# Mixture-of-experts block after attention: when GpSimd sends the experts' result rows

## The chip, the cores and the metric

The kernel runs on one core of one Trainium2 chip. The metric is the device time of one launch in microseconds (us). The kernel before takes 563.42 us (median of 3 runs, 561.5 to 564.76). The engines are called by these names: TensorE (PE in the profile), VectorE (DVE), ScalarE (ACT), GpSimd (POOL), and SyncE (SP), which here only starts DMA transfers.

## What is computed

4096 tokens of width 256 pass through an attention block with a residual, and then through a feed-forward block of 32 small experts, of which each token uses 4, beside one shared expert:

```python
x = x + _L0_xattn_ref(_layernorm(x), mask, ctx_2048, ctx_2048, wq, wk, wv, wo)
x = x + _L0_ffn_ref(_layernorm(x), router_weight, w_gate, w_up, w_down, sw_gate, sw_up, sw_down, sgate_w)

# inside _L0_ffn_ref, E, F, FS = (32, 96, 512), TOP_K = 4
probs = jax.nn.softmax(x @ router_weight.T, axis=-1)
topv, topi = jax.lax.top_k(probs, TOP_K)
topv = topv / jnp.sum(topv, axis=-1, keepdims=True)
g = jnp.einsum('th,ehf->etf', x, w_gate)
u = jnp.einsum('th,ehf->etf', x, w_up)
act = jax.nn.silu(g) * u
out = jnp.einsum('te,etf,efh->th', combine, act, w_down)
shared = jax.nn.silu(x @ sw_gate) * (x @ sw_up) @ sw_down
out = out + jax.nn.sigmoid(x @ sgate_w) * shared
```

## The kernel before

The program has three parts in time. First the attention, the router and the scattering: GpSimd sends each token's normalized row to four places of a DRAM table `sent`, ordered by expert. Then the expert loop, which this change touches. At last the shared expert's remaining products and the weighing of the experts' results.

In the expert loop the rows of `sent` are taken in 136 tiles of 128 rows, two tiles to a pair, 68 pairs (0 to 67). Every odd pair from 3 to 65 is mixed: its first tile holds four quarters of 32 rows, each for an expert of its own, and its weights are copied together beforehand (`gu_copy`, `dn_copy`). One pair goes through these steps:

- SyncE loads its rows into one of six buffers `loaded` (L366, L368).
- TensorE transposes them (L920), ScalarE copies the result to `gt` (L597).
- TensorE multiplies by gate and up (L944, L948), ScalarE applies SiLU to the gate (L603), VectorE multiplies gate and up into `act_e` (L1366, semaphore `act_e_ready`).
- TensorE transposes that product (L958), VectorE copies it (L1372, `act_et_ready`), TensorE multiplies by down (L972, L975, `down_psum`).
- VectorE copies the result from PSUM into `down_e`, one of four buffers of SBUF inside `arena2` (L1381, `down_ready`). The profile calls it arena.
- GpSimd starts two indirect DMA transfers for a pair (L480), one a tile. Each writes 128 rows to the places in DRAM (`returned`) that `back` names. They count up `down_sent`.

All engines run their own list in a fixed order, and wait on counting semaphores. VectorE's list for iteration `pair` is: the product of `pair` (L1366), the `down_e` copy of `pair - 4` (L1381), the copy of the transposed product of `pair - 1` (L1372), with the small steps that make `back` in the even iterations (L1395 to L1410) between them; in the odd iterations from 5 on two copies of down weights for a mixed pair (L1438) follow.

Two waits tie GpSimd's transfers to the rest. Before the copy of pair q + 4 into the same buffer, VectorE waits until both transfers of pair q have landed:

```python
                if pair >= DOWNS:
                    dve.wait_ge(down_sent[u], 32 * (pair // DOWNS))
```

And after the loop SyncE waits for all of `down_sent` (L372) before it loads the first results back for the weighing (L375). GpSimd has no other work during the loop and after it.

Of the kernel before, what the change touches and what calls it, by code (L numbers as in the profile page):

```python
# [35 lines left out]
def build_xattn_moe(nc, x, ctx, ctx_t, wq_t, wk_t, wv_t, wo_t, router_t, w_gate_up, w_down,  # L36
# [34 lines left out]
    with ExitStack() as stack:  # L71
# [181 lines left out]
        def wait(eng, name, count):  # L253
            if count > 0:
                eng.wait_ge(S[name], count)
# [47 lines left out]
        def _(sp):  # L303
# [51 lines left out]
            for pair in range(pairs):  # L355
                u = pair % RING
                first, size = column_of(pair), QUARTER if mixed(pair) else P
                _, at = nc.values_load_multi_w_load_instructions(
                    tile_row[0:1, first:first + (5 if mixed(pair) else 2)], engines=[mybir.EngineType.SP],
                    min_val=0, max_val=EXPERTS * tokens - size,  # L360
                    skip_runtime_bounds_check_because="a tile's first row is a row of an expert's "
                                                      "region, at most its count less a tile on")
                wait(sp, "gt_psum", pair - RING + 1)
                wait(sp, "back_ready", (pair - RING) // 2 + 1)
                for q in range(P // size):
                    sp.dma_start(loaded[size * q:size * q + size, u, 0, :].bitcast(F32), sent[bass.ds(at[q], size), :]) \  # L366
                        .then_inc(tile_in[u], 16)
                sp.dma_start(loaded[:, u, 1, :].bitcast(F32), sent[bass.ds(at[P // size], P), :]).then_inc(tile_in[u], 16)  # L368
# [15 lines left out]
        def _(pool):  # L384
# [87 lines left out]
            for pair in range(pairs):  # L472
                u = pair % DOWNS
                wait(pool, "back_ready", pair // 2 + 1)
                wait(pool, "down_ready", pair + 1)
                for s in range(2):
                    t = 2 * pair + s
                    if s == 1:
                        wait(pool, "act_e_ready", min(pair + 6, pairs))
                    pool.indirect_dma_start(  # L480
                        out=returned,
                        out_offset=bass.IndirectOffsetOnAxis(ap=back[:, t:t + 1], axis=0),
                        in_=down_e[u][:, s, :], in_offset=None).then_inc(down_sent[u], 16)

        @block.scalar
        def _(act):
# [121 lines left out]
            def experts_to_copy(pair):  # L608

                first = column_of(pair)  # L610
                more = 7 if mixed(pair + 2) else 0
                _, values = nc.values_load_multi_w_load_instructions(
                    tile_expert[0:1, first:first + 4 + more], engines=[mybir.EngineType.Activation],
                    min_val=0, max_val=EXPERTS - 1,
                    skip_runtime_bounds_check_because="a tile's first row over the rows of a region "
                                                      "is the number of an expert")
                copied_e[pair], copied_e[pair + 2] = values[0:4], values[7:11]
# [58 lines left out]
        def _(pe):  # L676
# [248 lines left out]
            def experts_of(pair):  # L925
                first = column_of(pair) + (4 if mixed(pair) else 0)
                _, values = nc.values_load_multi_w_load_instructions(
                    tile_expert[0:1, first:first + (1 if mixed(pair) else 2)], engines=[mybir.EngineType.PE],
                    min_val=0, max_val=EXPERTS - 1,
                    skip_runtime_bounds_check_because="a tile's first row over the rows of a region "  # L930
                                                      "is the number of an expert")
                return values
# [610 lines left out]
```

## Time and profile before

| what | value |
|---|---|
| median of three runs, without profile | 563.42 us (561.5 to 564.76) |
| span of the profiled execution, first to last instruction | 649.9 us |
| mean granted TensorE clock | 0.937 of full speed |
| GpSimd's transfers of the loop (L480) | 136, first at 324.9 us, last at 566.8 us |
| expert loop, by VectorE's products (L1366) | 314.0 to 550.4 us |

The page gives the span of the profiled execution and no other time of it. The span is 86.5 us longer than the median of the runs without a profile. A profiled execution is read for what waits for what, and for how long single instructions take. Its times are microseconds from the first instruction. Matmul ends are modelled.

### The profile page before, as it was taken

To read this page: it belongs to the slowest core of one execution; us is meant where nothing else is said; L and a number is where in the kernel's file an instruction comes from. 1 tells how busy PE (TensorE), PEld (TensorE's weight loads), DVE (VectorE), ACT (ScalarE), POOL (GpSimd) and SP (SyncE) were. 2 spreads that over 40 slices of the span, in tenths; PEclk is the share of its full clock that TensorE was granted. 3 is DMA by queue.
4 is the path that set the end of the run, shared out by engine and by line. 5 is a ranking of instruction groups with operands and counts; after the bars stand their busy time and mean duration, and the time that the engine had idled before them with its cause. 6 is when DMAs were issued, how large, how long until landed. Compare 5 with 4: busy or idle time off the path is not lost.

```text
span 649.9 us, 13112 instructions
## 1 busy us (share of the span) xinstructions
PE 575.3 (89%) x3884; PEld 435.9 (67%) x3884; DVE 353.5 (54%) x1169; ACT 251.0 (39%) x631; POOL 294.9 (45%) x502
## 2 busy tenths in 40 slices
PE   7999895985987867599999999899999998979997
PEld 7999784874876545255777666676677785455565
DVE  4468663663644662451445455454455545269985
ACT  4755451540533322001556455456555644101110
POOL 3011858158166688773055544555555555600000
PEclk8999987797798998799999989899999997979999
DMA  6578454253247194223345544455545551288863
GB/s 180 178 250 255 164 157 151 91 168 140 72 146 248 69 216 171 93 79 101 101 144 152 153 134 142 138 162 151 153 145 158 158 149 70 93 349 293 302 220 130
DMA packets 65956, 104.36 MB, mean 161 GB/s; under 512 B 9856, under 2 KB 52864, under 8 KB 65792
## 3 DMA queue, kind: packets, MB, share of 16 engines
q1 hardware_dynamic: 48160, 63.62, 32.9%
q0 software_dynamic: 12672, 35.14, 14.9%
q10 hardware_dynamic: 5056, 4.75, 2.3%
q8 instruction: 34, 0.56, 0.4%
q14 instruction: 34, 0.28, 0.2%
HBM read 59.84 MB, written 43.65 MB: 159 GB/s over the span
## 4 chain that ended last, share of the span: by engine, by line
PE 63%; another core or an unknown queue 13%; DVE 7%; issue 6%; ACT 4%; POOL 2%; DMA 2%; ACTq 1%; DVEq 1%; POOLq 0%; SPq 0%
PE bank L694 11%; PE bank L701 11%; PE bank L948 9%; PE bank L975 7%; PE bank L736 5%; PE bank L944 4%; PE bank L845 3%; PE bank L972 3%; PE bank L920 2%; PE bank L860 2%; PE bank L874 2%; POOL sent L444 1%; PE bank L958 1%; ACT hnt L625 1%
## 5 line engine op out<-in xcount | busy, mean ns | idle before, releaser
L480 POOL DMA_INDIRECT returned<-arena,back x136 | 130.7, 961 | 138.3 <-DVE arena L1366 63.4
L444 POOL DMA_INDIRECT sent<-rows,slot x128 | 125.2, 978 | 40.9 <-issue 28.2
L701 PE MATMUL bank<-hnt,ws_gu 128*128 128x512 f32 x256 | 117.7, 608 | 1.4 <-DVE arena L1381 1.4
L701 PEld LDWEIGHTS bank<-hnt,ws_gu 128*128 128x128 f32 x256 | 49.0, 195 | 55.6 <-issue 52.4
L948 PE MATMUL bank<-w_gu,arena 128*128 x416 | 85.8, 344 | 0.5 <-ACT arena L597 0.5
L948 PEld LDWEIGHTS bank<-w_gu,arena 128*128 128x128 f32 x416 | 66.8, 192 | 1.7 <-issue 0.8
L597 ACT COPY arena<-bank 128x512 f32<-128x512 f32 x68 | 39.4, 581 | 64.8 <-PE bank L920 35.1
L427 POOL TENSOR_TENSOR rstd<-var_eps,neg_half 128x4 f32<-128x4 f32 (+1 forms) x21 | 19.0, 907 | 91.6 <-DVE var_eps L1058 83.1
L1366 DVE TENSOR_TENSOR arena<-bank,arena 128x192 f32<-128x192 f32 x68 | 24.2, 355 | 65.8 <-ACT arena L603 51.7
L1381 DVE COPY arena<-bank 128x512 f32<-128x512 f32 x68 | 46.6, 685 | 22.8 <-remote 15.8
L505 ACT ACTIVATE act_t<-bank 128x512 f32<-128x512 f32 x24 | 14.3, 597 | 115.3 <-PE bank L701 86.5
L1484 DVE SCALAR_TENSOR_TENSOR resid<-arena,combine,resid 128x256 f32<-128x256 f32 x128 | 51.5, 476 | 9.1 <-DMA arena<-returned 9.1
L625 ACT COPY hnt<-w_gu 128x384 f32 x128 | 56.0, 514 | 0.0
L694 PE MATMUL bank<-w_hi_all,att_split 128*128 128x256 f32 x256 | 51.5, 304 | 3.0 <-issue 2.5
L694 PE MATMUL bank<-att_split,w_hi_all 128*128 128x256 f32 x256 | 46.1, 292 | 7.0 <-issue 5.7
L736 PE MATMUL bank<-ws_d,act_t 128*128 128x256 f32 x192 | 46.9, 405 | 4.7 <-DVE act_t L1075 3.5
L736 PEld LDWEIGHTS bank<-ws_d,act_t 128*128 128x128 f32 x192 | 39.1, 205 | 13.6 <-DVE act_t L1075 3.9
L920 PE MATMUL bank<-ident_r,loaded 128*128 128x128 f32 x272 | 45.3, 290 | 0.0
L603 ACT ACTIVATE arena<-bank 128x192 f32<-128x192 f32 x68 | 22.3, 328 | 53.4 <-PE bank L944 21.4
L694 PEld LDWEIGHTS bank<-att_split,w_hi_all 128*128 128x128 f32 x256 | 38.3, 200 | 5.9 <-issue 4.2
L694 PEld LDWEIGHTS bank<-w_hi_all,att_split 128*128 128x128 f32 x256 | 39.4, 201 | 3.6 <-issue 2.9
L920 PEld LDWEIGHTS bank<-ident_r,loaded 128*128 128x128 f32 x272 | 30.9, 142 | 10.4 <-issue 4.7
(188 smaller groups left out, 965.2 us busy)
## 6 DMA issues: line engine op xcount, KB each, us to landing
arena<-returned SPq DMA_DIRECT2D x16, 1024.0 KB, 6.7
loaded<-sent SPq DMA_DIRECT2D x104, 132.0 KB
w_gu<-w_gate_up SPq DMA_DIRECT2D x16, 384.0 KB
sent<-rows SPq DMA_DIRECT2D x4, 1056.0 KB, 6.4
loaded<-sent SPq DMA_DIRECT2D x128, 33.0 KB
resid<-x SPq DMA_DIRECT2D x16, 256.0 KB
att_plain<-ctx_t SPq DMA_DIRECT2D x16, 256.0 KB
att_plain<-ctx SPq DMA_DIRECT2D x16, 256.0 KB
```

The source lines that it names most:

```text
L444: pool.indirect_dma_start(out=sent, out_offset=bass.IndirectOffsetOnAxis(ap=slot[:, 2 * b + j, k:k + 1], axis=0), in_=rows[:, u, j, :], in ...
L480: pool.indirect_dma_start(out=returned, out_offset=bass.IndirectOffsetOnAxis(ap=back[:, t:t + 1], axis=0), in_=down_e[u][:, s, :], in_offs ...
L597: act.copy(gt[pair % 2].rearrange("p s c q -> p (s c q)"), gt_banks[pair % 2][:, :]) \
L625: last = act.copy(gu_copy[:, q, :, :], w_gu[:, :, bass.ds(copied_e[pair][q], 1), :] .rearrange("p c e f -> p c (e f)"))
L694: last = pe.matmul(out_view, stationary(s_part, c), moving(m_part, c), start=(n == 0 and c == 0), stop=(n == 2 and c == DC - 1))
L701: last = pe.matmul(bank[:, :], ws_gu[:, c, at:at + P], hnt[:, c, 512 * g:512 * g + 512], start=(c == 0), stop=(c == DC - 1))
L736: last = pe.matmul(sum_banks[t // 2][:, 256 * (t % 2):256 * (t % 2) + 256], act_t[:, f, P * t:P * t + P], ws_d[:, f, :], start=(f == 0 and ...
L920: last = pe.transpose(gt_banks[pair % 2][:, at:at + P].bitcast(F32R), loaded[:, u, s, P * c:P * c + P], ident_r[:, :])
L948: last = pe.matmul(view[:, s, :], rows_t[:, s, c, :], w_gu[:, c, bass.ds(e[s - 2 + len(e)], 1), :] .rearrange("p e f -> p (e f)"), start=( ...
L975: last = pe.matmul(bank[:, D * s:D * s + D], act[:, s, :], w_dn[:, bass.ds(e[s - 2 + len(e)], 1), :].rearrange("p e d -> p (e d)"), start= ...
L1381: dve.tensor_copy(down_e[u].rearrange("p s d -> p (s d)"), down_banks[pair % 2][:, :]) \
L1484: dve.scalar_tensor_tensor(tile, picked[i % YR][:, j, k, :], combine[:, t, k:k + 1], tile, ALU.mult, ALU.add) \
```

## The change

One condition is different. Before, the first transfer of every pair waits only for its own data, and the second also waits for VectorE's product six products on (`act_e_ready` at `pair + 6`, that is the product of pair + 5). Afterwards only the first transfer of every even pair has that wait. The other three of the four transfers of an even pair and the next odd pair have only the waits for their own data.

```diff
                 wait(pool, "back_ready", pair // 2 + 1)
                 wait(pool, "down_ready", pair + 1)
                 for s in range(2):
                     t = 2 * pair + s
-                    if s == 1:
+                    if pair % 2 == 0 and s == 0:
                         wait(pool, "act_e_ready", min(pair + 6, pairs))
                     pool.indirect_dma_start(
```

No instruction changes its place on any engine. Only the waits in GpSimd's list move. These are the first five transfers in the list of the kernel before, pairs 0, 0, 1, 1 and 2:

```order
L480 DMA returned<-arena,back 36864x256 [waits down_ready,back_ready]
L480 DMA returned<-arena,back 36864x256 [waits act_e_ready]
L480 DMA returned<-arena,back 36864x256 [waits down_ready,back_ready]
L480 DMA returned<-arena,back 36864x256 [waits act_e_ready]
L480 DMA returned<-arena,back 36864x256 [waits down_ready,back_ready]
```

And these are the same five in the list of the changed kernel:

```order
L480 DMA returned<-arena,back 36864x256 [waits act_e_ready,down_ready,back_ready]
L480 DMA returned<-arena,back 36864x256
L480 DMA returned<-arena,back 36864x256 [waits down_ready,back_ready]
L480 DMA returned<-arena,back 36864x256
L480 DMA returned<-arena,back 36864x256 [waits act_e_ready,down_ready,back_ready]
```

The wait on `act_e_ready` stands at one transfer in four, where it stood at one in two, and it stands ahead of the run and no longer inside each pair.

## Rows read from the trace of the kernel before

**Rows 1.** The page: span, busy time of GpSimd, chain that ended last.
```profile
span 649.9 us, 13112 instructions
...
PE 575.3 (89%) x3884; PEld 435.9 (67%) x3884; DVE 353.5 (54%) x1169; ACT 251.0 (39%) x631; POOL 294.9 (45%) x502
...
PE 63%; another core or an unknown queue 13%; DVE 7%; issue 6%; ACT 4%; POOL 2%; DMA 2%; ACTq 1%; DVEq 1%; POOLq 0%; SPq 0%
```

**Rows 2.** Busy time by stretch of the expert loop, with granted clock and DMA.
```profile
400.00:450.00 50.00, 46.21 (x388) 34.79 (x386) 24.51 (x82) 28.07 (x72) 25.97 (x29) 0.97 0.49 148
450.00:500.00 50.00, 48.13 (x410) 37.77 (x406) 26.74 (x92) 27.22 (x69) 27.88 (x29) 1.00 0.52 154
```

**Rows 3.** GpSimd's transfers (line 480) from 330 to 550 us, and their waits.
```profile
L480 POOL DMA_INDIRECT returned<-arena,back x121: 954/959/1067, 332.5 to 549.4; - x121
...
  DVE arena L1366: 62.7, 36
...
who waited for it (us, times):
busy tenths in 40 slices 0000000000000000000035544555555554000000
```

**Rows 4.** Timeline of one cycle of two pairs: start, duration, engine, line.
```profile
405.37 0.36 DVE L1366 TENSOR_TENSOR arena<-bank,arena 128x192 f32<-128x192 f32 x1 [1.48 <-ACT arena L603]
...
406.00 0.96 POOL L480 DMA_INDIRECT returned<-arena,back  x1 [2.20 <-DVE arena L1366]
...
407.02 0.35 DVE L1366 TENSOR_TENSOR arena<-bank,arena 128x192 f32<-128x192 f32 x1
...
407.27 0.96 POOL L480 DMA_INDIRECT returned<-arena,back  x1 [0.30 <-issue]
...
408.18 0.69 DVE L1381 COPY arena<-bank 128x512 f32<-128x512 f32 x1 [0.81 <-PE bank L975]
408.53 0.96 POOL L480 DMA_INDIRECT returned<-arena,back  x1 [0.30 <-issue]
...
409.79 0.96 POOL L480 DMA_INDIRECT returned<-arena,back  x1 [0.30 <-issue]
...
413.46 0.36 DVE L1366 TENSOR_TENSOR arena<-bank,arena 128x192 f32<-128x192 f32 x1 [0.84 <-ACT arena L603]
...
414.09 0.96 POOL L480 DMA_INDIRECT returned<-arena,back  x1 [3.34 <-DVE arena L1366]
```

**Rows 5.** Timeline of the last pairs' transfers and copies.
```profile
545.32 0.96 POOL L480 DMA_INDIRECT returned<-arena,back  x1 [0.30 <-issue]
...
550.45 0.35 DVE L1366 TENSOR_TENSOR arena<-bank,arena 128x192 f32<-128x192 f32 x1
...
550.69 0.96 POOL L480 DMA_INDIRECT returned<-arena,back  x1 [0.30 <-issue]
...
552.52 0.68 DVE L1381 COPY arena<-bank 128x512 f32<-128x512 f32 x1
...
559.53 0.96 POOL L480 DMA_INDIRECT returned<-arena,back  x1 [0.30 <-issue]
...
563.01 0.96 POOL L480 DMA_INDIRECT returned<-arena,back  x1 [2.51 <-DVE arena L1381]
```

**Rows 6.** Chain that ended last, after the loop: start, duration, what.
```profile
566.80 2.40 DMA returned<-arena,back
...
569.28 4.82 DMA arena<-returned
...
574.19 2.53 DVE resid L1484 x7
```

**Rows 7.** Timeline: copies of down weights (L1438) with a transfer beside them, and without.
```profile
402.84 0.96 POOL L480 DMA_INDIRECT returned<-arena,back  x1 [0.30 <-issue]
...
403.20 0.70 DVE L1438 COPY hnt<-arena 96x256 f32 x2 [0.83 <-issue]
...
412.14 0.48 DVE L1438 COPY hnt<-arena 96x256 f32 x2
...
415.16 1.08 PE L972 MATMUL bank<-hnt,slot_prod 96*32 96x256 f32 x8
```

**Rows 8.** Who waited for whom on TensorE, 315 to 552 us.
```profile
PE bank L972 <- DVE hnt L1438: 0.6, 1, 0.6
```

## The prediction

> **What bounds the kernel now.** I read the page first. TensorE is busy for 575.3 of 649.9 us and holds 63% of the chain that ended last; GpSimd holds 2% of it [rows 1]. Another 13% of that chain has no named releaser. The reader should see that GpSimd is no bound of the whole, and ask next whether it is one inside the expert loop. The view by stretches answers: in the middle of the loop TensorE is busy for 46.21 and 48.13 of 50 us, VectorE for 24.51 and 26.74, GpSimd for 25.97 and 27.88 [rows 2]. Then I asked for line 480 alone. 121 transfers take 0.954 to 1.067 us each on GpSimd, GpSimd itself stood waiting for VectorE's product for 62.7 us in 36 places, and the list of who waited for these transfers is empty [rows 3]. So in the loop the transfers are work that others release and nobody waits for. The one place where they are on the chain lies behind the loop: the last transfer starts at 566.80 and takes 2.40 us to land, then SyncE's load takes 4.82 us, then VectorE weighs [rows 6]. A change of when the transfers start can cost time in two ways only: at a buffer that VectorE wants to fill again before its transfer has landed, or at that last transfer.
>
> **What the change does in one cycle.** A cycle is an even and an odd pair. Take the one with VectorE's product of pair 26 at 405.37, of 27 at 407.02 and of 28 at 413.46 [rows 4]. A transfer that such a product releases starts 0.63 us after the product's start (406.00 less 405.37; 414.09 less 413.46 is the same), and transfers in a run follow each other every 1.26 us (407.27, 408.53, 409.79) [rows 4]. Before, the run is: second transfer of pair 21 at 406.00, both of pair 22 at 407.27 and 408.53, first of 23 at 409.79, and the second of 23 only at 414.09, after the product of 28 [rows 4]. Afterwards the run of pairs 22 and 23 waits for the product of 27. It starts at 407.02 + 0.63 = 407.65, and goes on at 408.91, 410.17 and 411.43. The third needs the `down_e` copy of pair 23, which ends at 408.18 + 0.69 = 408.87 [rows 4], in time. So three of the four move by +0.38 us and the fourth by 414.09 - 411.43 = 2.66 us to earlier. Where the two products lie further apart, the even pair's second transfer moves by up to a whole step of 1.26 us to later, since before it was released by the same product and had one transfer less ahead of it. That is the largest delay of a pair's landing in this scheme while the copies are in time. GpSimd's total work is unchanged: 4 transfers of 1.26 us, 5.05 us a cycle, in a cycle of 413.46 - 405.37 = 8.1 us here, and of 2 x 236.4 / 68 = 7.0 us on the mean (the last L1366 at 550.45 [rows 5], the first at 314.0 by the table above).
>
> **Step 1, buffers: 0 us.** A pair's transfers must have landed before VectorE's copy of the pair four on. For the landing I take the 2.40 us of the last transfer [rows 6]; other landings are not given in a view. The tightest place that I found before is pair 60: its second transfer starts at 545.32, has landed at 547.72, and the copy of pair 64 into its buffer starts at 552.52 [rows 5]. That is a slack of 4.80 us. Afterwards it starts 1.26 later, and 3.54 us remain. So this cost is zero, covered by 3.54 us. If a transfer landed 3.54 us later than I assume, in every cycle, VectorE would be late by up to 1.26 us a cycle more than before, 34 x 1.26 = 43 us at the very most. Nothing in the rows of the loop has anybody waiting for these transfers [rows 3], so I take 0.
>
> **Step 2, the end of the loop: 0 us, at most +0.4.** Before, the first transfer of pair 62 starts at 550.69 and seven more follow in a row, up to the second of pair 65 at 559.53. Then GpSimd waits 2.51 us for VectorE's copy and starts on pair 66 at 563.01 [rows 5]. Afterwards the run of pair 62 waits for the product of 67, at 550.45: 550.45 + 0.63 = 551.08. It is 0.39 us later, its eighth transfer starts at 559.92 and ends at 560.88, and pair 66 starts at 563.01 as before. The 2.51 us of idle time hide the 0.39. The last transfer stays at 566.80, and all of rows 6 with it. Without that gap, as could be in an execution in which TensorE delivers sooner, the 0.39 us would go through to the end whole. I keep +0.4 for the range.
>
> **Step 3, the start of the loop: 0 us.** The first transfer of pair 0 now waits as well. Its buffer is wanted again only four pairs on, and behind it in GpSimd's list there are only transfers.
>
> **Step 4, the waits themselves: 0 us.** In four transfers one wait on `act_e_ready` is left of two. A transfer with a wait already satisfied follows the one before it after 0.30 us of idle time [rows 4], and the new ones have no better row. GpSimd idles for half of the time anyway [rows 2].
>
> **Step 5, VectorE beside GpSimd: 0 us, at most some 7.** The two copies of down weights take 0.48 us together when no transfer runs, and 0.70 us when one started just before [rows 7]. So a transfer does cost VectorE up to 0.22 us there. Afterwards the run of four fills the 5.05 us behind the odd product, and these copies always fall into it; before, a part of them already did. Over 32 mixed pairs the upper bound is 32 x 0.22 = 7.0 us of VectorE, if none were hit before. But the copies are not on the path: in the cycle shown they end at 412.62 and TensorE wants them at 415.16 [rows 7], and TensorE waited for them once in the loop, for 0.6 us [rows 8]. I take 0. The Trainium skill, page SBUF — State Buffer, section "Who interferes with whom", has the rule that speaks against this change: a copy of VectorE in a two-port mode and GpSimd's writing of descriptors lock each other out for a whole instruction. By that rule a copy hit early in a transfer would wait out most of its 0.96 us, and the bound would be 32 x 0.96 = 31 us where the rows give 7.0; the trace shows 0.22 us for two copies, so I go by the rows.
>
> **Sum.** 0 + 0 + 0 + 0 + 0. Against its own time the profiled execution stays at 649.9 us of span. The runs without a profile have a median of 563.42 us, 86.5 us less, and I put the same zero on it: 563.4 us. The profile stretches the loop, so that all the slacks above could be some 13% smaller without it (563.42 / 649.9 = 0.87); 3.54 us becomes 3.1, and the conclusion stands. For the cycle, 7.0 x 0.87 = 6.1 us is still more than GpSimd's 5.05.
>
> **The rivals.**
>
> *Slower, by VectorE's copies.* The mechanism of step 5 with no cover: every mixed pair's copies are hit and TensorE waits for each. That gives 563.4 + 7.0 = 570.4 us, and with half of them 566.9. It decides once the cover between copy and product, 2.5 us in the cycle shown, falls under 0.22 us. Against it: rows 8. For it: the runs without a profile are denser, and the overlap with the copies is now in every cycle.
>
> *Slower, by the buffers.* The mechanism of step 1: transfers compete with SyncE's row loads for the same 16 DMA engines (busy for 0.49 to 0.52 of the time [rows 2]) and a run of four queues up behind itself, so that landings come over 3.5 us later than the 2.40 taken. If a quarter of the 34 cycles lost 1.26 us, that is +11 us, 574 us. Against it: four in a row is what the list does already in the cycle shown.
>
> *Faster.* The fourth transfer goes 2.66 us earlier, and then GpSimd and its queue are quiet until the next odd product, so that row loads and VectorE have that time to themselves. TensorE's idle time is 1.9 to 3.8 us in 50 [rows 2], at its mean 5.7% of 236 us = 13.4 us for the loop. A quarter of it, an amount that I chose, is 3.4 us: 560.0 us. Against it: no row has TensorE waiting for row loads, or VectorE for GpSimd.
>
> *The change does not act.* The third transfer of a run finds its `down_e` copy late and the run breaks in two. Then the times are near those of before: 563.4 us again.
>
> **How the numbers follow.** The bound between no change and a change is 0.5% of 563.42, 2.8 us, so 560.6 to 566.2 us (three runs of this kernel lie 3.3 us apart, so no smaller difference can be told from none). No change by steps 1 to 5, with the +0.4 of step 2 and the case in which the change does not act: 0.66, own range 561.5 to 565.5 us. Slower by the copies 0.13, by the buffers 0.05, together 0.18. Faster 0.16. The likeliest case gives 563.4 us. The range goes down to 559.5 for the faster case and up to 568 us for half of the copies, and leaves out the buffers' case and the whole 7 us.
>
> **What the changed profile would show.** Starts of line 480 in runs of four, the first 0.63 us behind an odd pair's product, 1.26 us apart; nobody waiting for line 480 in the loop; GpSimd's idle time put down to line 1366 about as long, in half as many places. The gap before pair 66 smaller by 0.4 us, and the last transfer about 16.4 us behind the last product, as before. VectorE's copies of line 1438 at 0.48 to 0.70 us for two, more often the latter, and no wait of TensorE for them. I would be wrong if VectorE's line 1381 waited for a landing, if TensorE's wait for line 1438 grew to over 3 us, or if TensorE's own gaps moved for a reason that no row here has.

## The result: 0.3% slower

The changed kernel takes 564.24 us in the median of 20 runs, the kernel before 563.07 us in the median of 20 runs beside it. The ratio is 1.0032, with a 95% interval of 1.0019 to 1.0046: about 1.8 us slower (the medians alone lie 1.2 us apart). I had forecast no change. The time lies inside the range given, and under the bound of 0.5%, but it did move, and the sum of zeros has a step that failed.

One thing must be known to read what follows: in some batches every execution of every kernel took 634 to 687 us at a granted clock of 0.90 to 0.95, in the others 559 to 567 us at 0.98 to 0.99, but for one run of the changed kernel of 875.43 us at 0.557. The profile in front of the prediction has a span of 649.9 us. The profile of the changed kernel has 563.2 us, and a new one of the unchanged kernel (h1_before, below) has 559.8 us in a run timed at 561.86 us. So it is not the profiling that stretched the first one. The last two can be laid side by side. Of the page of the changed kernel, span, busy time and chain:

```profile
span 563.2 us, 13112 instructions
...
PE 535.8 (95%) x3884; PEld 417.0 (74%) x3884; DVE 355.0 (63%) x1169; ACT 251.0 (45%) x631; POOL 294.8 (52%) x502
...
PE 75%; POOL 12%; issue 3%; DVE 3%; DMA 3%; SPq 2%; POOLq 1%; DVEq 0%
```

Of the page of the kernel before at the same speed:

```profile
span 559.8 us, 13112 instructions
...
PE 76%; POOL 10%; DMA 5%; issue 3%; DVE 3%; SPq 2%; POOLq 0%; ACT 0%; DVEq 0%; ACTq 0%
```

Against [rows 1] the reader should see two things. The 13% of the chain without a releaser are gone, and GpSimd's share of the chain is 10%, not 2%. Right behind the last product the chain of the execution of 649.9 us went through stretches without a named releaser (the longest 4.19 us) and VectorE's late copies of line 1381:

```profile
557.28 4.19 another core or an unknown queue
...
561.56 0.70 DVE arena L1381
```

There the chain of h1_before has GpSimd's transfers.

The transfers of the changed kernel do go in fours. Line 480, its waits and who waited for it:

```profile
L480 POOL DMA_INDIRECT returned<-arena,back x136: 954/960/969, 270.7 to 481.2; - x136
its engine sat idle before it (us, times) until:
  DVE arena L1366: 39.5, 12
...
who waited for it (us, times):
```

Nobody in the loop waits for them, as before [rows 3]. So I looked behind the loop first. Timeline of GpSimd's transfers in the changed kernel, from the last one of pair 55 through those of pair 56 and the first of pair 62 to the second of pair 67, with VectorE's product of pair 61, that of pair 67 (its last), and the copy of pair 56:

```profile
446.19 0.68 DVE L1381 COPY arena<-bank 128x512 f32<-128x512 f32 x1
...
449.17 0.36 DVE L1366 TENSOR_TENSOR arena<-bank,arena 128x192 f32<-128x192 f32 x1 [0.80 <-ACT arena L603]
...
465.70 0.36 DVE L1366 TENSOR_TENSOR arena<-bank,arena 128x192 f32<-128x192 f32 x1 [0.46 <-ACT arena L603]
...
447.14 0.96 POOL L480 DMA_INDIRECT returned<-arena,back  x1 [0.30 <-issue]
450.31 0.96 POOL L480 DMA_INDIRECT returned<-arena,back  x1 [2.20 <-DVE arena L1366]
453.39 0.96 POOL L480 DMA_INDIRECT returned<-arena,back  x1 [2.12 <-issue]
454.65 0.96 POOL L480 DMA_INDIRECT returned<-arena,back  x1 [0.30 <-issue]
...
467.30 0.96 POOL L480 DMA_INDIRECT returned<-arena,back  x1 [0.30 <-DVE arena L1381]
...
479.95 0.96 POOL L480 DMA_INDIRECT returned<-arena,back  x1 [0.30 <-issue]
481.21 0.96 POOL L480 DMA_INDIRECT returned<-arena,back  x1 [0.30 <-issue]
```

The same places in the kernel before at the same speed (h1_before):

```profile
443.75 0.36 DVE L1366 TENSOR_TENSOR arena<-bank,arena 128x192 f32<-128x192 f32 x1 [1.96 <-ACT arena L603]
444.11 0.68 DVE L1381 COPY arena<-bank 128x512 f32<-128x512 f32 x1
...
447.09 0.36 DVE L1366 TENSOR_TENSOR arena<-bank,arena 128x192 f32<-128x192 f32 x1 [0.80 <-ACT arena L603]
...
463.62 0.36 DVE L1366 TENSOR_TENSOR arena<-bank,arena 128x192 f32<-128x192 f32 x1 [0.46 <-ACT arena L603]
...
444.38 0.96 POOL L480 DMA_INDIRECT returned<-arena,back  x1 [0.92 <-DVE arena L1366]
445.65 0.96 POOL L480 DMA_INDIRECT returned<-arena,back  x1 [0.30 <-issue]
449.22 0.96 POOL L480 DMA_INDIRECT returned<-arena,back  x1 [2.61 <-DVE arena L1381]
...
457.46 0.96 POOL L480 DMA_INDIRECT returned<-arena,back  x1 [0.92 <-DVE arena L1366]
...
463.78 0.96 POOL L480 DMA_INDIRECT returned<-arena,back  x1 [0.30 <-issue]
...
477.69 0.96 POOL L480 DMA_INDIRECT returned<-arena,back  x1 [0.30 <-issue]
```

In the changed kernel the data of pair 56 is copied by 446.87, but its first transfer waits for the product of pair 61 and starts at 450.31. From 453.39 on 23 transfers follow each other every 1.26 us to the end without a gap. GpSimd never catches up, and a start that is late stays late. Before, pair 56 starts at 445.65, right behind the transfer ahead of it.

The last product of the changed kernel comes 465.70 - 463.62 = 2.08 us later, and of these 256.48 - 254.72 = 1.76 us are there at the first product of the loop, which the change does not touch; so distances from the last product are what counts. The last transfer comes 481.21 - 465.70 = 15.51 us behind it, against 477.69 - 463.62 = 14.07: 1.44 us. The second transfer of pair 56 comes 12.31 us ahead of the last product, against 14.40. Of these 2.09 us GpSimd's idle time at 457.46 (0.92 instead of 0.30 us) gives 0.62 back to the changed kernel, which has no such gap.

Where do the 2.09 us come from? One transfer more stands between the product and this one: 1.26 us, the shift that the prediction named. The rest has two sources. A second transfer of a pair that waited for a product started 0.63 us behind the start of that product, as in [rows 4] (in h1_before 0.62 to 0.64 us in 37 of 40 cases: 444.38 less 443.75 above). A first transfer of a pair that waited for one started 1.14 us behind it (450.31 less 449.17; 1.13 to 1.15 us in the 11 cases in which the changed kernel's trace has GpSimd idle for the product). That is 0.51 us more, and why it is so is open. The remaining 0.32 us belong to a late start of the second transfer of pair 56 that no wait explains, 1.82 us in the changed kernel (2.12 of idle time instead of 0.30) and 1.50 before (449.22, with the product at 447.09 + 0.63 = 447.72).

What would be left without that late start? An estimate from these rows: with steps of 1.26 us and the waits at 1.14 us behind their products, the first transfer of pair 62 would then start on its own wait, 465.70 + 1.14 = 466.84, instead of at 467.30. Before, it starts 463.78 - 463.62 = 0.16 us behind the last product. So the wait of pair 62 for the last product would by itself cost 1.14 - 0.16 = 0.98 us; the backlog from pair 56 is later still and makes it 1.44. No run at this speed moved the one without the other.

What follows the last transfer, in the chain of the changed kernel: landing, SyncE's load, the first weighing, then the product (L1075) that stands behind the weighing in VectorE's list and that TensorE wants:

```profile
481.21 2.39 DMA returned<-arena,back
...
483.69 4.89 DMA arena<-returned
...
488.67 2.53 DVE resid L1484 x7
...
491.93 0.61 DVE act_t L1075
```

TensorE's waits from 460 to 500 us, changed kernel:

```profile
PE bank L736 <- DVE act_t L1075: 4.3, 1, 4.3
```

And before (h1_before):

```profile
PE bank L736 <- DVE act_t L1075: 2.6, 1, 2.6
```

The delay of 1.44 us shows up as 1.7 us more of TensorE's wait. From the start of the last transfer to the end of the span it is 563.2 - 481.2 = 82.0 us in the one and 559.8 - 477.7 = 82.1 us in the other. In this pair of traces the delay of the last transfer goes to the end whole. Single traces scatter here: the same distance is 82.1 to 83.3 us in the other traces of this speed below, but for one of 81.1 us (h3_before_free_end).

### The profile page after: what moved, and what is told of

The parts are those of the page before. It is cut to its first block, busy times and chain, and to the rows that moved or that the text cites. A ratio compares the mean times of both kernels' runs of the same rounds, so it can differ in the third digit from the quotient of the medians.

```text
span 563.2 us, 13112 instructions
## 1 busy us (share of the span) xinstructions
PE 535.8 (95%) x3884; PEld 417.0 (74%) x3884; DVE 355.0 (63%) x1169; ACT 251.0 (45%) x631; POOL 294.8 (52%) x502
## 4 chain that ended last, share of the span: by engine, by line
PE 75%; POOL 12%; issue 3%; DVE 3%; DMA 3%; SPq 2%; POOLq 1%; DVEq 0%
PE bank L694 16%; PE bank L948 12%; PE bank L701 10%; POOL sent L444 9%; PE bank L975 9%; PE bank L944 4%; PE bank L736 3%; PE bank L920 3%; PE bank L845 3%; PE bank L972 3%; PE bank L860 2%; PE bank L874 2%; POOL pause L453 2%; PE bank L958 2%; PE bank L986 1%
## 5 line engine op out<-in xcount | busy, mean ns | idle before, releaser
L701 PE MATMUL bank<-hnt,ws_gu 128*128 128x512 f32 x256 | 115.7, 601 | 0.0
L948 PE MATMUL bank<-w_gu,arena 128*128 x416 | 83.6, 338 | 1.0 <-ACT arena L597 1.0
L1381 DVE COPY arena<-bank 128x512 f32<-128x512 f32 x68 | 46.6, 686 | 11.1 <-PE bank L975 11.1
L694 PE MATMUL bank<-w_hi_all,att_split 128*128 128x256 f32 x256 | 48.6, 292 | 0.0
L694 PEld LDWEIGHTS bank<-w_hi_all,att_split 128*128 128x128 f32 x256 | 37.1, 190 | 0.8 <-issue 0.8
```

The lines of the kernel that those rows point to most:

```text
L694: last = pe.matmul(out_view, stationary(s_part, c), moving(m_part, c), start=(n == 0 and c == 0), stop=(n == 2 and c == DC - 1))
L701: last = pe.matmul(bank[:, :], ws_gu[:, c, at:at + P], hnt[:, c, 512 * g:512 * g + 512], start=(c == 0), stop=(c == DC - 1))
L948: last = pe.matmul(view[:, s, :], rows_t[:, s, c, :], w_gu[:, c, bass.ds(e[s - 2 + len(e)], 1), :] .rearrange("p e f -> p (e f)"), start=( ...
L1381: dve.tensor_copy(down_e[u].rearrange("p s d -> p (s d)"), down_banks[pair % 2][:, :]) \
```

## The experiments

Two theories. *End*: the loss is the late start of GpSimd's last unbroken run. *Loop*: transfers in fours slow VectorE's copies or TensorE within the loop. All kernels below compute the whole reference. Ratios are to the kernel before, run in the same batch.

### First batch: the rule undone at one end or the other

**e1_before**: the kernel before, unchanged.

> The kernel before, unchanged, for a profile beside which the changed kernel's can be read. Theory end (the changed kernel is late because GpSimd's last unbroken run of transfers starts later, and the last transfer is on the path): the last L480 starts 13.5 to 14.5 us behind VectorE's last product (15.5 us in the changed kernel), also in a run without gaps, and the products of the loop stand at the same times within 0.5 us. Theory loop (transfers in fours slow VectorE's copies or TensorE inside the loop): the last product comes 1 to 2 us sooner after the first than in the changed kernel, and the last transfer the same 15.5 us behind it.

**e2_after_free_end**, on the changed kernel:

```diff
-                    if pair % 2 == 0 and s == 0:
+                    if pair % 2 == 0 and s == 0 and pair < 54:
```

> The changed kernel, but from pair 54 on no transfer waits for a product. Theory end: the whole loss is undone and perhaps more, since the last run starts as soon as its data is there: ratio to the kernel before 0.994 to 0.999. Theory loop: 54 of 68 pairs still go in fours with their wait, so most of the loss stays: ratio 1.002 to 1.003.

**e4_no_pace**, on the kernel before:

```diff
-                    if s == 1:
-                        wait(pool, "act_e_ready", min(pair + 6, pairs))
```

> The kernel before with no wait on a product at any transfer; each goes when its data is in down_e. Theory end: faster than before by what GpSimd is ahead at the end, 1 to 3 us: ratio 0.994 to 0.999. Theory loop (how the transfers lie in a cycle matters to VectorE and TensorE): the pace is lost, ratio over 1.001.

**e6_before_then_after**, on the kernel before:

```diff
-                    if s == 1:
+                    if s == 1 if pair < 54 else (pair % 2 == 0 and s == 0):
```

> The wait as before up to pair 53, and as in the changed kernel from pair 54 on. Theory end: all of the loss is here, ratio 1.002 to 1.004. Theory loop: a fifth of the loss, ratio 1.000 to 1.001.

Measured: the kernel before took 669.71 us in the median (659.21 to 676.46), the profiled e1_before 658.0 us of span. e2_after_free_end 0.9954 (0.9886 to 1.0022), e6_before_then_after 0.9949 (0.9891 to 1.0007), e4_no_pace 1.0235 (1.0163 to 1.0307). The first two can't tell the theories apart. In e1_before the last transfer comes 16.50 us behind the last product, where theory end had expected 13.5 to 14.5 us. GpSimd before pair 66:

```profile
568.48 0.96 POOL L480 DMA_INDIRECT returned<-arena,back  x1 [0.30 <-issue]
572.02 0.96 POOL L480 DMA_INDIRECT returned<-arena,back  x1 [2.58 <-DVE arena L1381]
```

It is the gap of [rows 5] again, 2.58 us. In h1_before and in the changed kernel's trace it does not exist.

### Second batch: again

**f1_before**, **f2_after_free_end** and **f6_before_then_after** are e1, e2 and e6 unchanged.

> The kernel before, unchanged, for a profile at the speed of the runs shown (563 us; the last batch ran at 660 to 670 us). Theory end: the last L480 starts 13.5 to 14.5 us behind VectorE's last product, where the changed kernel has 15.5 us, and the products stand where they do in the changed kernel within 0.5 us. Theory loop: the loop from the first to the last product is 1 to 2 us shorter than in the changed kernel, and the last transfer is the same 15.5 us behind it.

> The changed kernel, but from pair 54 on no transfer waits for a product. Theory end: the whole loss is undone, ratio to the kernel before 0.994 to 0.999. Theory loop: most of the loss stays, ratio 1.002 to 1.003.

> The wait as before up to pair 53, and as in the changed kernel from pair 54 on. Theory end: all of the loss is here, ratio 1.002 to 1.004. Theory loop: a fifth of the loss, ratio 1.000 to 1.001.

Measured: before 646.84 us (636.85 to 657.85), f2 1.0111 (1.0018 to 1.0204), f6 0.9956 (0.9908 to 1.0004). The same kernel gave 0.9954 in the batch before and 1.0111 here, so from the times alone I draw nothing. In the trace of f1_before (span 636.1 us) the gap before pair 66 is absent: GpSimd's last run goes without a gap from the second transfer of pair 61, and the last transfer comes 14.23 us behind the last product, within what theory end had.

The traces at this speed do show something about theory loop. From the first product to the last the loop takes 233.2 to 238.4 us in the ten traces in which the second transfer of each pair waits up to pair 53, 239.9, 240.6 and 243.9 us in the three whose transfers go in fours (j3_after_first_weighing_later, f2_after_free_end, e2_after_free_end), and 251.6 us in e4_no_pace. With one trace a run this is no proof, and its cause stays open, but theory loop is not refuted for executions of 634 us and more.

### Third batch: the same two, at 561 us

> The same kernel as in the last batch, since there the kernel before itself ran at 637 to 676 us and its spread hid a third of a per cent. From pair 54 on no transfer waits for a product. Theory end: ratio to the kernel before 0.994 to 0.999. Theory loop: ratio 1.002 to 1.003.

> The wait as before up to pair 53, as in the changed kernel from there on. Theory end: ratio 1.002 to 1.004, as the changed kernel itself. Theory loop: ratio 1.000 to 1.001.

Measured: before 560.97 us (559.81 to 563.33). **g2_after_free_end 0.9999 (0.9986 to 1.0013)**, **g6_before_then_after 1.0042 (1.0029 to 1.0056)**. At this speed the 54 pairs in fours cost nothing that can be measured; the waits from pair 54 on, seven in the new place for fourteen in the old, cost all of it. Theory loop falls for executions of 561 us. Theory end is right on g6 (1.002 to 1.004 expected); for g2 it had expected 0.994 to 0.999, and the gain over the kernel before did not come.

The traces say the same. GpSimd in g6_before_then_after, pair 56 and the last transfer:

```profile
450.27 0.95 POOL L480 DMA_INDIRECT returned<-arena,back  x1 [2.62 <-DVE arena L1366]
453.35 0.96 POOL L480 DMA_INDIRECT returned<-arena,back  x1 [2.13 <-issue]
...
481.17 0.96 POOL L480 DMA_INDIRECT returned<-arena,back  x1 [0.30 <-issue]
```

In g2_after_free_end:

```profile
447.64 0.96 POOL L480 DMA_INDIRECT returned<-arena,back  x1 [0.30 <-issue]
449.92 0.96 POOL L480 DMA_INDIRECT returned<-arena,back  x1 [1.32 <-DVE arena L1381]
...
478.88 0.96 POOL L480 DMA_INDIRECT returned<-arena,back  x1 [0.30 <-issue]
```

The last products start at 465.66 and 464.91, so the last transfer comes 15.51 and 13.97 us behind. TensorE's wait for L1075 is 4.3 us in g6, as in the changed kernel, and in g2:

```profile
PE bank L736 <- DVE act_t L1075: 2.8, 1, 2.8
```

### Fourth batch: what the wait is for

**h1_before** is the kernel before, **h4_no_pace** is e4. **h3_before_free_end**, on the kernel before:

```diff
-                    if s == 1:
+                    if s == 1 and pair < 54:
```

> The kernel before, unchanged, for a profile at 560 to 564 us, to lay beside those of the changed kernel (last transfer 15.52 us behind the last product, TensorE waiting 4.3 us for VectorE's L1075) and of the kernel with a free end (13.97 us, 2.8 us). Theory end: 14.0 to 14.6 us and 2.8 to 3.4 us. Theory loop: 15.5 us and 4.3 us, with a loop 1.5 us shorter.

> The kernel before, but from pair 54 on no transfer waits for a product. Theory end: GpSimd's last run starts a little sooner than before, by at most 0.6 us from the times of the changed kernel's trace: ratio 0.998 to 1.000. A rival (the waits have no part in the time of the kernel before at all): 1.000 within 0.001. They can hardly be told apart; the trace's distance from last product to last transfer does: 14.0 us or less against before's own.

> No transfer waits for a product. Theory end alone (only when the last run starts counts): as the last one, ratio 0.998 to 1.000. Theory loop (where the transfers lie in a cycle counts too, and the wait keeps them from a bad place): over 1.002, with the last transfer as early behind the last product as in the kernel with a free end, and a longer loop.

Measured: before 561.87 us (560.15 to 563.43), h3 1.0001 (0.9984 to 1.0017), h4 1.0010 (0.9996 to 1.0023). h1_before has 14.07 us, as theory end said, and a wait of 2.6 us, a little under the 2.8 to 3.4 expected. h3 and h4 both have 13.97 us and 2.6 us. From the first product to the last the loop takes 208.9 to 209.9 us in all six traces of this speed, whatever the waits. Taking the wait away altogether gains nothing and costs at most 0.2% at this speed. The wait of the kernel before is about as good as none. In the one batch at 670 us the kernel without it was 2.4% slower (1.0163 to 1.0307), with the longest loop of all traces; that was not repeated.

### Fifth and sixth batch: one wait alone, and the path behind the loop

**j1_one_wait** and **k1_one_wait**, on the kernel before (the same waits; k1 shown):

```diff
-                    if s == 1:
+                    if s == 1 or pair == 56:
```

**j4_one_wait_later**: this one wait for the product of pair 62 (`act_e_ready` at 63). **j2_before_first_weighing_later** and **k2_before_first_weighing_later**, on the kernel before, and **j3_after_first_weighing_later**, on the changed one:

```diff
-        TURNS = ((0, 1, 0, 3), (1, 1, 0, 3), (1, 1, 0, 2), (1, 1, 1, 0))
+        TURNS = ((0, 0, 0, 3), (1, 1, 1, 3), (1, 1, 0, 2), (1, 1, 1, 0))
```

`TURNS` gives, for each group of the shared expert's work, how many pairs of tiles are weighed behind each of its four products. The edit moves the first weighing behind the last of them.

> The kernel before with one wait more: the first transfer of pair 56 also waits for product 61, as in the changed kernel. Nothing else differs. Theory end: this one wait starts the last run later, and from the times of the kernel before's trace the last transfer comes 0.9 to 1.5 us later; ratio 1.0015 to 1.004. Rival (it takes the pattern of fours over the last 14 pairs, not one late start): 1.000 within 0.001.

> The same one wait, but for product 62, about 4 us later. Theory end: the last transfer 5.0 to 5.5 us later than in the kernel before, and TensorE waits as much longer for VectorE's L1075: ratio 1.008 to 1.010. If something behind the loop has slack, less: 1.004 or so. Rival: 1.001 or under.

> The kernel before, with the first weighing of two tiles moved behind the last of the four products of the shared expert of its group (TURNS 0,0,0,3 and then 1,1,1,3), so that no product that TensorE waits for stands behind the first results' load. If the late transfers cost time through TensorE's wait for L1075 (2.6 us in the kernel before, 4.3 in the changed one), that wait goes and the kernel is faster: ratio 0.995 to 0.998. If VectorE's weighing as a whole is the bound behind the loop, 0.999 to 1.001.

> The changed kernel with the same move. If the path from GpSimd's last transfer goes through TensorE's wait for L1075 only, the change costs nothing any more: the same ratio as the kernel before with the move, within 0.001. If it goes through VectorE's weighing as well, 0.002 to 0.003 above it, as the changed kernel stands to the one before.

> The same single wait as j1_one_wait (the first transfer of pair 56 also waits for product 61), since that batch ran at 640 to 666 us with a spread that hides it. Theory end: last transfer 0.9 to 1.5 us later than in the kernel before, ratio 1.0015 to 1.004. Rival (the pattern of fours over the last 14 pairs): 1.000 within 0.001.

> The same kernel as j2: before, with the first weighing behind the last of the group's four products. If TensorE's wait for L1075 (2.6 us in the kernel before) is on the path: the wait gone, ratio 0.995 to 0.998. If VectorE's weighing is the bound: 0.999 to 1.001.

Measured, with the kernel before at 645.35 us (641.63 to 665.63) and then 653.15 us (642.06 to 661.26): j1 0.9986 (0.9926 to 1.0047), j4 1.0058 (0.9983 to 1.0133), j2 0.9919 (0.9841 to 0.9997), j3 1.0037 (0.9973 to 1.0102), k1 0.9877 (0.9788 to 0.9966), k2 0.9961 (0.9899 to 1.0024). Both batches ran long, and their spread is several times what was to be measured. j2 and k2 both lie under 1, and TensorE's wait for L1075 in k2's trace is:

```profile
PE bank L701 <- DVE act_t L1075: 1.2, 1, 1.2
...
PE bank L736 <- DVE act_t L1075: 0.4, 1, 0.4
```

But k1 lies under 1 as well, with a wait added, and in the traces of j1 and k1 TensorE's wait at line 736 for L1075 is only 0.5 and 0.6 us, without the move. So this is no proof of a gain. Whether one wait at pair 56 is enough, and whether a later first weighing makes a better kernel, was not settled.

## Why the prediction was wrong, step by step

**What bounds the kernel.** The two places where a delay could cost were the right ones: a buffer, or the last transfer. The second is where it cost.

**What the change does in one cycle.** Right in its order: runs of four, 1.26 us apart, released by an odd pair's product. Wrong by 0.51 us in the release: I took 0.63 us from second transfers of a pair, and the new wait stands at first transfers, which started 1.13 to 1.15 us behind the product. That the largest shift named there, 1.26 us, is near the 1.44 us at the end is luck; it was not what step 2 counted.

**Step 1, buffers.** Right at 0: VectorE's L1381 waited for TensorE alone in the changed kernel's loop, and the rival by the buffers had nothing for it.

**Step 2, the end of the loop. This step failed, in three places.** It said that 2.51 us of idle time hide 0.39 us, and that without the gap "the 0.39 us would go through to the end whole". First, the gap: it is 2.51 us in [rows 5] and 2.58 us in e1_before, and absent in f1_before, in h1_before and in the changed kernel. I had seen that the profiled span was 86.5 us over the median, put it down to the profile, and put one factor of 0.87 on all slacks. But the profiled h1_before has a span of 559.8 us. The difference is not spread evenly; this slack did not shrink by 13%, it was absent. Second, the release. The same sum at this speed, with 0.63 us, gives 0.63 - 0.16 = 0.47 us, near the 0.39; with the 1.14 us of a first transfer it is 0.98 us. Third, the backlog. I took the last run to begin at pair 62, where it does in [rows 5]. With TensorE on time it begins at pair 56 in the changed kernel: 2.09 us at the second transfer of pair 56, 1.44 us at the last transfer. The term was 0 with a bound of 0.4 us; it measured 1.44 us in the traces and 0.32% (1.8 us) in the timing, 0.42% (2.4 us) in g6. The interval of the timing, 1.1 to 2.6 us, holds the 1.44; that of g6, 1.6 to 3.1 us, just does not. The some 0.4 to 1 us that are left have no cause here.

**Steps 3 and 4.** No cost was seen in the loop: g2 has all the moved waits up to pair 52 and stands at 0.9999. But step 4 said that the new waits need no price of their own, and the 0.51 us at a first transfer is one; at pairs 56 and 62 it counts.

**Step 5, VectorE beside GpSimd.** Right at 0. The 64 copies of line 1438 take 0.28 us in the median and 0.53 at most in the changed kernel, 0.28 and 0.51 before, and TensorE never waited for one in the changed kernel (0.3 us once before). The slower rival by the copies, to which I gave 0.13, is refuted by g2 at the speed of the timed runs. The rule of the Trainium skill, SBUF — State Buffer, "Who interferes with whom", would at its bound have cost 31 us; what the runs show of it in time is nothing.

**The faster rival.** The fourth transfer does come earlier, and nothing came of it. From the first product to the last it is 209.2 us, against 208.9 before.

## What to carry to other kernels

Before you cost an edit at nothing because idle time covers it, ask whether the profiled execution is one of those that are timed: where its span is 15% over the median, a gap in it may not exist at the speed that is timed, and one factor for all slacks doesn't mend that. Take the time from a release to a start from an instruction in the same place of the list: here it was 0.63 us for the second transfer of a pair and 1.14 us for the first. An engine that nobody waits for in a loop can still carry a backlog out of the loop; then follow its last unbroken run back to where it starts, because a delay there goes to the end, less the idle time that the other kernel has further on (here 2.09 us less 0.62). A new wait that only paces an engine should end some iterations before the loop does: without the seven last ones the loss was gone (g2). The old wait cost nothing there (h3, 1.0001).

## What was not expected of the hardware

In all 20 traces the second transfer of pair 56 starts later than its waits explain, always this one. In the changed kernel it has no wait at all and GpSimd idles 2.12 us before it, with 0.30 us before its neighbours. It is 2.12 or 2.13 us in 13 traces, of long and of short executions; 1.32 us in g2; and 2.61 to 3.37 us in the six in which the transfer itself waits for the product of pair 61 and the one ahead of it does not, in each 1.50 or 1.51 us more than that wait explains. The profile names no releaser for it in nine of them ("issue"), VectorE's copy of line 1381 in ten, and its product in one. No packet of the queues for instructions (kind "instruction" on the page) falls between 446 and 454 us in the changed kernel's trace. In h1_before it reaches nobody, since transfers further on wait for later products anyway (0.34 us of idle time before the second of pair 57, 0.92 us before the second of pair 59). In the changed kernel it is the backlog, by the estimate above 0.46 of the 1.44 us. Its cause stays open.

The 0.51 us between first and second transfers of a pair was not expected either. In h4_no_pace the 40 first transfers before which GpSimd idled for more than 0.33 us started 0.75 to 0.77 us behind the end of their pair's copy; second transfers that waited for a product started 0.27 us behind its end (0.63 less 0.36).
